# Two attention layers on one NeuronCore: where second-layer steps put their side work on TensorE

## The reference

```python
# first layer: 16 heads of 64
h = layernorm(x, gamma, beta)
Q, K, V = h @ Wq, context @ Wk, context @ Wv
x = x + (softmax(Q K^T) * 64 ** -0.5 @ V) @ Wo + bo
# second layer: 16 heads of 32
xn = x * rsqrt(mean(x * x) + 1e-5) * norm_w
q, k, v = xn @ wq, context @ wk, context @ wv
q, k = unit_length(rotate(q)), unit_length(rotate(k))
x = x + (softmax(q k^T * sqrt(32)) @ v) @ wout
```

## Time and profile before

| | us |
|---|---|
| median of 3 runs (3315.68 to 3317.42) | 3315.94 |
| the profiled execution's own time | 3319.18 |
| its span in the profile | 3317.4 |

### The profile page before, as it was taken

The page is one execution under the profiler, slowest core; times in us unless marked ns, Lnnn a source line. Parts: engine busy times, 40 slices in busy tenths (PEclk is TensorE's granted clock), DMA queues, the critical chain, the costliest instruction groups (busy, mean ns, idle before and its releaser), DMA issues.

```text
span 3317.4 us, 73642 instructions
## 1 busy us (share of the span) xinstructions
PE 3093.1 (93%) x31708; PEld 1565.2 (47%) x31708; DVE 2385.6 (72%) x2804; ACT 1409.6 (42%) x1728; POOL 499.0 (15%) x221
## 2 busy tenths in 40 slices
PE   5999999899999999988999999998999999999897
PEld 3555555444355555544345555454434455555441
DVE  3677776787777776678777777668876767766877
ACT  2333333456433333355643333345563333334565
POOL 1000002343000000335100000033410000013440
PEclk8999999999999999999999999999999999999999
DMA  3001010201111010011111110101112010100001
GB/s 109 19 21 25 21 25 16 58 24 37 45 50 28 21 25 21 22 54 24 36 48 49 25 25 21 25 19 56 28 33 72 22 27 21 25 21 22 19 16 36
DMA packets 178409, 107.32 MB, mean 32 GB/s; under 512 B 81452, under 2 KB 147116, under 8 KB 178088
## 3 DMA queue, kind: packets, MB, share of 16 engines
q1 hardware_dynamic: 178088, 102.60, 11.7%
HBM read 93.12 MB, written 9.42 MB: 31 GB/s over the span
## 4 chain that ended last, share of the span: by engine, by line
PE 82%; DVE 9%; issue 4%; ACT 3%; DMA 1%; SPq 1%; DVEq 0%; POOL 0%; ACTq 0%; POOLq 0%
PE o_acc L663 19%; PE scores L651 19%; PE work L691 13%; PE work L686 11%; PE work L713 9%; PE work L619 5%; DVE acc L810 4%; PE work L706 2%; ACT probs L740 2%; PE work L696 2%; DVE tile_max L791 1%; DVE resid L895 1%; DVE stats L830 1%; PE work L701 1%; PE work L723 1%
## 5 line engine op out<-in xcount | busy, mean ns | idle before, releaser
L740 ACT ACTIVATE probs<-scores 128x1024 f32<-128x1024 f32 x1024 | 996.4, 1023 | 481.6 <-PE scores L651 472.2
L810 DVE TENSOR_TENSOR acc<-acc,probs 128x1024 f32<-128x1024 f32 x768 | 983.8, 1304 | 21.4 <-DVE acc L810 1.8
L791 DVE TENSOR_REDUCE tile_max<-work 128x2 f32<-128x1024 f32 x496 | 607.2, 1224 | 523.5 <-PE work L619 519.9
L663 PE MATMUL o_acc<-probs,v_tok 128*64 128x512 f32 (+1 forms) x4096 | 778.5, 611 | 0.3 <-ACT probs L740 0.3
L925 POOL TENSOR_TENSOR inv<-sumsq,power 128x16 f32<-128x16 f32 x64 | 231.2, 3613 | 2066.7 <-DVE sumsq L876 2066.6
L713 PE MATMUL work<-wo,o_sum 128*32 128x512 f32 (+1 forms) x2072 | 401.5, 602 | 41.7 <-issue 28.4
L651 PE MATMUL scores<-q_high,k_high 32*128 32x512 f16 (+1 forms) x2048 | 309.1, 392 | 77.1 <-ACT probs L740 55.9
L663 PEld LDWEIGHTS o_acc<-probs,v_tok 128*64 128x64 f32 (+1 forms) x4096 | 165.6, 122 | 349.7 <-issue 334.5
L651 PE MATMUL scores<-q_high,k_low 32*128 32x512 f16 (+1 forms) x2048 | 303.6, 384 | 0.0
L651 PE MATMUL scores<-q_low,k_high 32*128 32x512 f16 (+1 forms) x2048 | 303.0, 383 | 0.0
L895 DVE TENSOR_TENSOR resid<-work,resid 128x512 f32<-128x512 f32 x384 | 261.8, 685 | 45.3 <-PE work L713 44.9
(11 more groups left out here) (76 smaller groups left out, 2660.3 us busy)
## 6 DMA issues: line engine op xcount, KB each, us to landing
recip<-rows_dram SPq DMA_DIRECT2D x380, 64.0 KB, 2.2
stage<-in_x_dram SPq DMA_DIRECT2D x8, 1024.0 KB, 6.6
wq<-in_L_xattn_Wq_dram SPq DMA_DIRECT2D x32, 256.0 KB, 2.7
resid<-in_x_dram SPq DMA_DIRECT2D x8, 1024.0 KB, 5.3
wo<-in_L_xattn_Wo_dram SPq DMA_DIRECT2D x32, 256.0 KB, 2.7
out_dram<-resid SPq DMA_DIRECT2D x8, 1024.0 KB, 4.4
wk<-in_L_xattn_Wk_dram SPq DMA_DIRECT2D x32, 192.0 KB, 2.4
wv<-in_L_xattn_Wv_dram SPq DMA_DIRECT2D x32, 192.0 KB, 2.5
```

Of the source, the lines that this page charges most:

```text
L663: mm = pe.matmul(o_acc[h * d:(h + 1) * d, :], v_tok[par][:, kt, h * d:(h + 1) * d], probs[:, unit_slot(t, n, kt, h // 2), h % 2, :], start ...
L740: act.activation(probs[:, no % RING, :, :], scores[:, unit_banks(t, n, kt, u), :], ACT.Exp, scale=(1.0, float(D1) ** 0.5 / QK_SCALE ** 2)[ ...
L791: dve.tensor_reduce(tile_max[:, qt, :, n:n + 1], maxima_banks(e), AX.X, ALU.max, negate=True).then_inc(dve_freed, 1)
L810: dve.tensor_tensor(a[:, heads, :], before, probs[:, unit_slot(t, n, kt, u), :, :], ALU.add).then_inc(add_ok, 1)
```

## The change

For a step with a single key tile and no maxima entries, so only in the second layer, the default order puts the side entries ahead of the step's values. The scores of the next step still come before both. VectorE's call of `run`, which passes `on_vector`, is as it was. The fourth turn's steps that hold maxima for the next batch (all but the first three of its 16) keep the old order; in the last batch there are none, so all 16 change.

```diff
-        def run(rowmax, scored, blocks, entry, order=lambda st: (st.first + st.early, st.fill + st.rest)):
+        def fill_first(st):
+
+            if len(st.kts) == 1 and not st.first + st.rest:
+                return st.early + st.fill, []
+            return st.first + st.early, st.fill + st.rest
+
+        def run(rowmax, scored, blocks, entry, order=fill_first):
```

## The result

The changed kernel takes 3338.29 us, the median of four runs (3336.16 to 3340.70), against 3316.03 (3315.68 to 3317.42) for the kernel before on the same chip. The direction was forecast; the amount is twice what was, and lies above the range. The profiled executions are 17.3 us apart, 3336.44 against 3319.18.

A forecast was written before the change was run, and what follows sets the result against it. TensorE, busy 93% of the 3317.4 us span, was taken as the bound. The terms 3.3 + 3.5 + 0.5 + 0.55 + 3.7 = 11.55, about 11.5 us on 3315.94, gave 3327.4 us; range 3316 to 3336.

The forecast's parts named there:

- the fall: Rival: the clock halves after the longer wait before xt, turn 1 half 0 step 0; 6 us more, 3333; chance 0.12.
- 2.11 brought no fall: Argument against the clock rival: TensorE's 2.11 us wait before xt in the profiled kernel was followed by no clock fall.
- Rows 10: Profile rows: after TensorE worked 0.09 us in 3.00, the granted clock was 0.50 in the 6 us that followed.
- Case 1: Turn 1 half 0 step 0: xt waits for the row norm, values go behind; 0.82 a batch, 3.3 us more.
- shape term: Tile shape changes on TensorE: one more in 43 steps, one fewer in 12, 0.12 each; 3.7 us more.
- Case 2: Turn 1 half 1 step 4: out waits on k_high behind the exponentials, values go behind; 0.88 times four, 3.5 us.
- Case 3: Turn 1 half 0 step 2: qr must wait for the copies to hT; 0.12 four times, 0.5 us more.
- Case 4: Last batch, turn 3: out is fixed by DMAs from sums, so the scores come later; 0.55 us once, hidden in last half.
- Waits that start in side work: Most waits before L713: the whole chain runs 0.88 earlier and the values follow; nothing gained or lost, cost 0.
- rows 6's place: Where qr feeds squares, VectorE rotates and scales, and out waits 1.64; sign: still 1.6 us, now ahead of the values.
- Nothing to see: Rival: waits starting in scores are covered by ScalarE-bound steps and shape changes even out; 3317; chance 0.18.
- The side work's readers set the pace: Rival: earlier transposes before k_high let ScalarE start sooner; 8.8 us less, 3307; chance 0.10.

The follow-up runs named there:

- e9: The kernel before with the new order in turn 1 half 0 step 0 alone, plus 12 filler products ahead of xt's wait in each batch: 3312.03 us, 0.9999.
- e2: The kernel before with the new order in turn 1 half 0 step 0 alone: 3327.60 us, 1.0037 of the kernel before.
- e1: The changed kernel, but turn 1 half 0 step 0 keeps values first: 3326.26 us, 1.0035 of the kernel before.
- e7: The kernel before with the new order only in 33 steps outside step 4 whose side work starts with out and ends with a transpose: 3319.29 us, 1.0016.
- e4: The changed kernel, but turn 1 half 1 step 4 keeps values first: 3336.71 us, 1.0074 of the kernel before.
- e6: The kernel before with the new order only in six places whose side work feeds a wait; steps that wait keep values first: 3303.91 us, 0.9971.
- e10: e6 with 7 filler products ahead of xt's wait in each batch: 3303.95 us, 0.9974 of the kernel before.
- e3: The changed kernel with 20 filler products ahead of xt's wait in each batch: 3333.69 us, 1.0055 of the kernel before.

## Why the prediction was wrong

**The step that failed is the clock's.** The forecast had the wait before `xt` right, 3.0 us for 3.10, and put what follows it at full speed; the fall was a rival with a chance of 0.12 and a price of 1.5 us a batch. It came in four batches of four, with 6.8 us of low clock in each (in the third in two parts, one ahead of the wait), and cost 9.5 us in all, 2.4 a batch (the changed kernel's trace against e9's; e2's gives 7.5). Two arguments were wrong. "2.11 brought no fall" was read from one execution, and e1 and e7 show falls behind that very wait; and it says nothing about 3.0. Rows 10 did say something: they are a wait of 2.92 us, and the clock was at 0.50 from 658.16, 2.1 us into it, before TensorE had worked again:

```profile
655.00:658.10 3.10, 1.04 (x12) 0.13 (x8) 1.99 (x5) 1.94 (x2) 3.02 (x4) 1.00 0.34 85
658.20:664.90 6.70, 5.94 (x36) 1.28 (x40) 6.70 (x6) 1.94 (x2) 5.96 (x3) 0.50 0.13 39
```

That is 1.04 us of work in 3.10, and the forecast made a wait of this length four times. The other wrong argument is the price, halved because ScalarE would hide part of it. It hides nothing here: `xt`, `den` and values are a run of TensorE work with ScalarE waiting, and the whole of it was doubled; only what lies in the wait costs nothing (0.9 of the 6.8 us in the first batch). With 9.5 added the forecast's 11.5 would have been 21, against 22.3.

**Case 1, the values behind the wait:** forecast 3.3, measured 3.2 (0.80 in each batch, e9). These steps start with a transpose and end with `den`, so the forecast's shape term took 0.12 off each: 0.70 with it, for 0.80. Right but for 0.1 a batch.

**Case 2, `k_high`:** forecast 3.5, measured 3.4, 0.86 in each of four steps. Right as a cost of the change. The reason was incomplete: it isn't tied to that step, since holding it moves 0.86 to the next `den` in three batches (e4).

**Case 3, `qr` behind `hT`:** forecast 0.5, measured 1.1, 0.27 in each. I took the end of ScalarE's copy as the moment when TensorE may start; 0.15 lies between in the changed kernel's first batch (649.10 and 649.25). Mis-sized.

**Case 4:** forecast 0.55, measured 0.28, and 0.62 in step 4 of the last half, where I had expected it hidden. Neither can be told from chance: the same two steps, in the old order, differ from the kernel before by 0.00 and 0.42 in e6 and by 0.85 and -0.58 in e9. The end of VectorE's chain was not tested.

**Waits that start in side work:** forecast 0. Right as a balance, rows 6's place has a wait of 1.77 for 1.64, the shape term apart from that; and e6 shows that the two sides of the balance are real, 0.86 each.

**Tile shapes:** forecast 0.12 in 43 steps and the same back in 12, 3.7 us. Measured 0.14 more in 34 of the 43 and some 0.14 less in 8 of the 12; the other four are the `xt` steps. Right. The Trainium skill (TensorEngine Tiling (Array Packing), Key Properties) says that a change of tiling mode drains TensorE. E7's rows agree as far as they go: a step with one change more takes 0.14 us more. Without this term the forecast would have been nearer to no effect.

**The rivals.** "Nothing to see" fell with the result, 22.3 us clear of its noise, and with e6 and e7. "The side work's readers set the pace" fell as an account of this change, but its mechanism is what e6 lives on, in the six places where the awaiting step keeps its order.

**The range** was too narrow above: it ended at 3336 because the clock was allowed 6 us. What the profiled executions don't share is also larger than I took it: the changed kernel's runs spread over 4.5 us, and e1 to e10 over up to 15.5. Falls of the clock that come and go at places with no edit are one source, seen from trace to trace; that they are all of it is not shown.

## What to carry to other kernels

A reorder within a step has two ends: work moved ahead reaches its readers sooner, and whatever stood before a wait no longer fills it. Price both at each wait, and change only the steps that feed a wait, not those that wait: the same edit cost 22 us applied to 217 steps and gained 9 us applied to six places. And when an edit lengthens a wait of TensorE, look at what it does right behind the wait; work there may run at half the clock. One trace in which the clock held doesn't say that it always will.

## What the runs showed of the hardware

A wait of TensorE of 3.10 us before `xt`, with 1.04 us of work in the 3.20 us up to 638.20, came with a granted clock of 0.50 (1.2 GHz) that began inside the wait, in three batches of four; in the fourth the clock was low ahead of the wait, which was 2.34 us, and fell again behind it. In each batch the low clock took 6.8 us in all. Over four kernels with this order it fell in or right behind the wait in 16 of 16 steps. With 7, 12 or 20 products of no use in the wait, it fell there in 0 of 16. With the old order and a wait of 2.1 us (1.4 in one step of e6) it fell behind the wait in 4 of 16 steps (two in e1, two in e7). What decides between falling and not falling at 2.1 us stays open.

A product of 128x128 in float32 takes 0.22 us of TensorE, two records of 0.11 (e3: 20 in 4.57 us, to the first transpose). A step with one change of tile shape more takes 0.14 us more (e7: 4.41 for 4.27).
